# Zeroing a message table part by part from one queue, and a node load moved ahead of the weights, in a graph-convolution kernel

## The reference

```python
h = jnp.maximum(_layernorm(x, axis=-1), 0.0)
z = jnp.concatenate([h[src], h[dst], edge_attrs], axis=-1)
m = jax.nn.sigmoid(z @ W_f + b_f) * jax.nn.softplus(z @ W_s + b_s)
message = jax.ops.segment_sum(m, src, num_segments=100000)
mean, var = message.mean(0), message.var(0)
out = x + h + (message - mean) * rsqrt(var + 1e-5) * gamma + beta
```

## Time and profile before

| | |
|---|---|
| timed runs, median (lowest, highest) | 1071.09 us (1069.85, 1071.23) |
| profiled execution, span from the first to the last instruction | 1087.2 us |
| what lies around that span in the profiled execution | not given by the page; its own time is at least the span |
| busy: POOL, DVE, PE, ACT | 735.4, 742.1, 579.7, 536.9 us |
| bytes moved by DMA | 176.02 MB |

### The profile page before, as it was taken

The page is one execution under the profiler, slowest core; times in us unless marked ns, Lnnn a source line. Parts: engine busy times, 40 slices in busy tenths (PEclk is TensorE's granted clock), DMA queues, the critical chain, the costliest instruction groups (busy, mean ns, idle before and its releaser), DMA issues. The chain is left out here.

```text
span 1087.2 us, 11011 instructions
## 1 busy us (share of the span) xinstructions
PE 579.7 (53%) x2442; PEld 406.6 (37%) x2442; DVE 742.1 (68%) x1551; ACT 536.9 (49%) x1185; POOL 735.4 (68%) x652
## 2 busy tenths in 40 slices
PE   0321754456553756664564556575636679844332
PEld 0121542335442534542352335454424479610000
DVE  3523766658766678757587666677566568789788
ACT  1131664556464656454565645664546556333332
POOL 7774777777878787777778777878787710650620
PEclk9855576765676565557666755655676579855555
DMA  7994443545443434434344334334333579589999
GB/s 280 416 402 151 111 124 75 123 94 123 104 120 77 125 59 79 85 56 83 62 83 78 86 53 86 62 78 82 63 76 58 153 290 410 195 254 414 416 404 387
DMA packets 88145, 176.02 MB, mean 162 GB/s; under 512 B 42561, under 2 KB 49285, under 8 KB 79663
## 3 DMA queue, kind: packets, MB, share of 16 engines
q1 hardware_dynamic: 34903, 111.46, 29.0%
q0 software_dynamic: 42880, 20.09, 16.5%
q10 hardware_dynamic: 10328, 44.12, 10.0%
HBM read 107.12 MB, written 68.50 MB: 162 GB/s over the span
## 5 line engine op out<-in xcount | busy, mean ns | idle before, releaser
L584 POOL DMA_INDIRECT m_buf<-in_x_dram,m_buf x384 | 368.4, 959 | 118.3 <-issue 111.6
L597 POOL DMA_INDIRECT msgs_dram<-sums,target x184 | 289.2, 1572 | 69.0 <-issue 56.0
L1164 PE MATMUL ps_all<-sums,m_last 128*128 128x64 f32 x920 | 152.2, 338 | 26.9 <-issue 23.7
L707 DVE TENSOR_REDUCE m_last<-late 128x24 f32<-128x1536 f32 (+1 forms) x49 | 85.3, 1741 | 113.8 <-ACT late L978 84.4
L1164 PEld LDWEIGHTS ps_all<-sums,m_last 128*128 128x128 f32 x920 | 145.9, 251 | 38.3 <-issue 35.4
L1117 PE MATMUL ps_all<-ident,m_last 128*128 128x128 f32 x49 | 21.2, 432 | 225.3 <-ACT sums L1036 212.0
L1138 PEld LDWEIGHTS ps_all<-m_buf 128*128 128x128 f32 x392 | 93.8, 328 | 50.0 <-issue 50.0
L1036 ACT ACTIVATE sums<-ps_all 128x256 f32<-128x256 f32 x46 | 17.6, 382 | 187.3 <-remote 187.3
L1027 ACT ACTIVATE m_last<-m_last,one_col 128x512 f32<-128x512 f32 x196 | 107.6, 550 | 1.6
L678 DVE SCALAR_TENSOR_TENSOR m_buf<-ps_all,m_buf 128x1024 f32<-128x1024 f32 x97 | 93.2, 960 | 19.3 <-remote 15.6
L827 DVE TENSOR_TENSOR y_kept<-ps_all,m_buf 128x256 f32 (+1 forms) x196 | 82.5, 422 | 26.6 <-remote 13.6
(11 more groups left out here) (171 smaller groups left out, 1076.1 us busy)
## 6 DMA issues: line engine op xcount, KB each, us to landing
m_buf<-msgs_dram SPq DMA_DIRECT2D x38, 1024.0 KB, 8.4
m_buf<-in_x_dram SPq DMA_DIRECT2D x48, 512.0 KB
out_dram<-m_buf ACTq DMA_DIRECT2D x20, 1024.0 KB, 10.8
msgs_dram<-y_kept SPq DMA_DIRECT2D x11, 1536.0 KB
m_buf<-src_rows_dram SPq DMA_DIRECT2D x47, 256.0 KB
y_spill_dram<-y_kept ACTq DMA_DIRECT2D x19, 512.0 KB
y_kept<-y_spill_dram SPq DMA_DIRECT2D x8, 1024.0 KB, 14.8
msgs_dram<-y_kept ACTq DMA_DIRECT2D x5, 1536.0 KB
```

The source lines that it names most:

```text
L584: pool.indirect_dma_start(xg[:, n % G_SLOTS, 2 * j + c, :], None, x, bass.IndirectOffsetOnAxis(ap=ids[:, c, n * TILES + j:n * TILES + j + ...
L597: pool.indirect_dma_start(msgs, bass.IndirectOffsetOnAxis(ap=target[:, n % UNROLL, j:j + 1], axis=0), comb[:, n % COMB_SLOTS, j, :], None, ...
L707: dve.tensor_reduce(row_ssq[:, rows], sq[:, rows, :], AX.X, ALU.add).then_inc(ssq_done, 1)
L1164: pe.matmul(ps_c[:, j, :], same_of(b, j, j + 1)[:, 0, :], msg_of(g)[:, b, :], start=(b == 0 and not begun), stop=(b == j), skip_group_chec ...
```

## The change

- The table is cut into 12 parts of 64 rows for each partition (2.1 MB, 512 packets of 4096 bytes) in place of 16.
- ACT issues part 0 alone, at the place where it issued parts 0 and 1. Its later loop is gone.
- SP issues the other eleven, and waits before each part k until `table_zeroed` has reached 16 k, which is when parts 0 to k-1 have landed. Parts 1 and 2 stand ahead of load 3, parts 3 and 4 ahead of load 4, parts 5 to 7 ahead of load 5, parts 8 to 11 behind it. The last pair follows without a wait, and the source rows of groups 2 and 3 follow that.
- SP's load of group 0 stands ahead of the 14 loads of weights and biases in place of behind them.

```diff
-ZERO_PARTS = 16
-ZERO_EARLY = 5
-ZERO_FIRST = 2
+ZERO_PARTS = 12
+ZERO_FIRST = 1
+ZERO_AT = ((1, 3), (3, 5), (5, 8), (8, 12))
...
+    def zero_table(eng, k):
+
+        n = whole // ZERO_PARTS
+        eng.dma_start(m_rows[:, k * n:(k + 1) * n, :].rearrange("p (n r) f -> p n (r f)", r=BULK),
+                      zeros[:, :].unsqueeze(1).to_broadcast([P, n // BULK, BULK * F])
+                      ).then_inc(table_zeroed, 16)
...
-        for u in range(SLOTS):
+        load(Group(0, 0))
+        load_weights()
+        for u in range(1, SLOTS):
             load(Group(0, u))
-        sp.wait_ge(zeros_set, 1)
-        done = ZERO_EARLY
         for u in range(SLOTS, UNROLL + 1):
-            end = min(ZERO_PARTS, 2 * ZERO_EARLY + 1 + 3 * (u - SLOTS))
-            for k in range(done, end):
-                zero_table(k)
-            done = end
+            for k in range(*ZERO_AT[u - SLOTS]):
+                sp.wait_ge(table_zeroed, 16 * k)
+                zero_table(sp, k)
             if u < UNROLL:
                 load(Group(0, u))
+        sp.dma_start(m_rows[:, whole:N_ROWS, :],
+                     zeros[:, 0:(N_ROWS - whole) * F].rearrange("p (r f) -> p r f", f=F)).then_inc(table_zeroed, 16)
+        over = (N_REST + DUMP) // FILL
+        sp.dma_start(msgs[P * N_ROWS:NODES + DUMP, :].rearrange("(p r) f -> p (r f)", p=FILL),
+                     zeros[0:FILL, 0:over * F]).then_inc(table_zeroed, 16)
...
         for k in range(ZERO_FIRST):
-            zero_table(k)
+            zero_table(act, k)
...
-        for k in range(ZERO_FIRST, ZERO_EARLY):
-            zero_table(k)
```

More of the change, by code:

```diff
@@ L464, in stage_one @@
     EDGES_TURN = STEPS + 1
+    whole = N_ROWS // BULK * BULK
+    def zero_table(eng, k):
[3 more added lines that the diff above has]
+                      ).then_inc(table_zeroed, 16)
     def sync(sp):
@@ L476, in sync, with load_weights @@
                          v[0:P - E_REST].rearrange("(p t) -> p t", t=1)).then_inc(ids_rest, 16)
[L478 to L486, removed]
+        def load_weights():
+            sp.wait_ge(w_cleared, 1)
+            for c, (w, b) in enumerate(((w_f, b_f), (w_s, b_s))):
+                cols = slice(c * F, (c + 1) * F)
+                sp.dma_start(w_z[0:F, cols], w[0:F, :]).then_inc(w_loaded, 16)
+                sp.dma_start(w_z[F:2 * F, cols], w[F:2 * F, :]).then_inc(w_loaded, 16)
+                for j in range(TILES):
+                    sp.dma_start(w_e[j * EF:(j + 1) * EF, j, cols], w[2 * F:2 * F + EF, :]).then_inc(w_loaded, 16)
+                sp.dma_start(b_row[:, cols], b.rearrange("(a f) -> a f", a=1).to_broadcast([SPLIT, F])
+                             ).then_inc(w_loaded, 16)
         def load_nodes(g):
```

## The result

The kernel after takes 1088.3 us (1087.5 to 1088.5) against 1070.5 us (1069.9 to 1071.2): ratio 1.0163, with 95% interval 1.0149 to 1.0178. It is 17.8 us slower. The spans of the two profiled executions do not show it: 1086.8 us after, 1087.2 before.

The account below looks back on a forecast made before the run. POOL's first add was taken to bound the kernel. Table: 17 + 70.4 + 2.1 + 13 = 102.5 us, 9.0 later than a timed 93.5, so 1071.1 + 9.0 = 1080 us; range 1067 to 1088, the forecast's own 1075 to 1088.

Parts of the forecast that it names:

- What bounds the kernel: Stage one: POOL never rests, so a delay of its first add moves the kernel's end one for one.
- The lag as a matter of the profiled execution: Waiters 25 and 22 us behind PE's ends; most of POOL's 13.0 us wait before its first add absent from timed runs.
- The first rival: Late wake-ups of waiting engines are in timed runs too; first add moves 106.54 to 102.5, time 1067; chance 0.20.
- It was zero at about 89.5: Kernel before: zeroed table ready 4 us before POOL asks at 93.5, dated by the DMA share falling to 0.47.
- The last pair 0.84 MB, 2.1 us: End of the zeroing: the two last zero copies after the eleven parts, priced at 2.1 us.
- The price of a part: SP's zero parts, one in flight: 5.1 us transfer plus gap, 6.4 us each, 70.4 us for 11.
- the 13 us of other traffic: Gathers, loads and spills beside the zeros: 6.7 MB, 16 us, a fifth fitting into the gaps, so 13 us.
- the 0.3 us for landing, wait and wake: Share of the gap between two zero parts, beside 1.0 us from issue to first bytes.
- The start at 17 us: SP's issue of zero part 1, after ids, weights and loads 0 to 2: 17 us (14 to 20).
- the worth of the node rows: Group 0's load ahead of the weights: pipeline starts 5 to 8 us earlier, nothing on the path.
- The hole: POOL's wait between its 72nd gather and first add; after the change ended by a landing of zeros at 98 to 110 us.
- The third rival: SP's queue: load 5 waits for DVE's step 3, four parts behind it; table at 133, up to 1097; chance 0.09.

## Why the prediction was right in its direction and half short in its size

- **What bounds the kernel** was right: a late first add of POOL goes one for one into the time (the table above).
- **The lag as a matter of the profiled execution** was right. Two further profiles of the same kernel are without it, with spans of 1068.8 and 1068.7, and the 33 timed executions beside the experiments have spans of 1067.3 to 1070.7. The first rival, that it is in timed runs too, is dead: it asked for 1067, and an edit to the table alone took 6.3 us off the kernel before, where ACT's copy at 105 would have hidden it. The copy was put at about 72 us without the lag; it stands at 74. That a recording block pushes back on the engines, as the Trainium skill has it in "NOTIFIC — the notification-queue block", section 7.1, remains a possible cause. No run here shows the block. The density of records alone does not explain the lag: it stood in one profile of three, and the profile without it recorded more instructions from 20 to 88 us (94 on PE, 89 on DVE and 51 on ACT, against 56, 63 and 29). What made that one execution slow is open.
- **"It was zero at about 89.5" was the step that failed.** I took the fall of the DMA share to 0.47 for the end of the zeros. Behind it the share went on at 0.27 to 0.13 until 98 us, in the end two engines still writing the 424 KB. Without the lag that end is at 101.5. So a timed run of before already waited some 7.8 us, and its first add stood at 101.6, not at 93.5. This made the forecast loss too large by 8.1 us: 4.5 (98 in place of 93.5) were to be read in that profile, 3.6 were the lag's lighter traffic and were not.
- **"The last pair 0.84 MB, 2.1 us" was the term most mis-sized**: I priced it at the rate of 16 engines, and half of it runs on two. From the last part's issue to the first add it was 18.6 us, and 6.4 + 1.2 + 2.1 = 9.7 by my terms: 8.9 too few. Spreading that copy took 9.1 us off the time.
- **The price of a part** was right, and what was low is the first of them. 6.4 us and 13 / 11 = 1.2 of other traffic make 7.6; nine of the ten intervals between issues average 7.7. The first is 12.7, 5.1 more: I spread the 13 us of other traffic evenly, and an estimated 4 us of it (1.7 MB at 410 GB/s) had been issued just ahead of part 1. No row stood behind the 0.3 us for landing, wait and wake, but the whole cost of a wait, 1.3 us, came out as 14.7 / 11 = 1.3. The estimate in the prediction by the Trainium skill's formula ("DMA: Bandwidth & Descriptors", "Anatomy of one DMA"; 6.8 in place of 6.4) would give 8.0 with the other traffic, a little more than the 7.7. That section fits the formula to DMAs issued from GpSimd, and these came from SP; no part was alone on the engines here, so no run shows it by itself.
- **The start at 17 us** was right (17.03), and so was the worth of the node rows: nothing.
- Sum: table at 102.5 predicted, 117.5 measured, 15.0 late (6 of it up to the last part's issue, 9 behind); the start of the comparison 93.5 predicted, 101.6 measured, 8.1 late. The difference was 9.0 and became 15.9 by the profiles and 17.8 by the times. The hole was to end between 98 and 110 us and ended at 117.5. The range reached up to 1088 and the time is 1088.3, at its very edge. That it came so near is luck: the two errors worked against each other. With the table of before read right, the forecast would have been about 1072; with the table of after alone, 1071.1 + 24.0 = 1095.
- The third rival (SP caught behind a load) did not come: load 5 went out right behind part 7, at 69.9 us, as did loads 3 and 4 behind parts 2 and 4, so none of the three waited for DVE.

The best kernel of the study is the kernel before with its last zero copy cut for 16 engines, at 1064.0 us.

## What to carry to other kernels

A bulk transfer kept at one piece in flight pays the issue-to-landing gap for every piece; two in flight give it back, and if nothing waits for the lighter traffic there is nothing to gain. Read a DMA stretch to its last byte: here a share of 0.13 was two engines at work, and one copy over 106 partitions at the end of the zeros cost as much as five of the eleven waits, or more. Where the span of a profile is longer than the timed runs, profile the same kernel again before any wait in it is believed.

## What was not expected of the hardware

- A copy of 424 KB from 106 partitions ran on alone for some 9 us at the end of the zeros, at 43 to 53 GB/s. It took 6.3 us of the time of the kernel before, and 9.1 of the kernel after.
- In one profile of three, DVE waited 3.5 us for its own result with the DMA engines at a share of 0.03, and the span was 18.4 us longer; the same profile moved fewer bytes beside the zeros, so it erred in both directions.
- Small weight loads were slow to issue beside large copies of the other queue: four loads of 8 KB took 4.52 us with a third part of zeros in flight and 1.98 in the kernel before, where the two early parts were nearly done. With parts 2 to 4 behind the stores of the source rows they took 5.55.
